# Sums of the looked-up feed-forward weights: from POOL's additions to accumulating DMAs in SBUF

## The chip, the core and the metric

The kernel runs on one core of one Trainium2 chip. The metric is the device time of one execution in microseconds (us), shorter is better.

## What is computed

One transformer block on x, 1024 tokens of 256 channels: a layer norm, attention with 16 heads of 128 and linear position penalties (ALiBi), and beside it a feed-forward part whose three weight matrices are looked up in a table of 16 values.

```python
def _ghost_linear(x, idx, lut):
    w = lut[idx]                                  # int codes 0..15 -> weights
    return jnp.einsum('bsh,oh->bso', x, w)

xn = _layernorm(x)
qkv = xn @ qkv_w + qkv_b
scores = einsum(q, k) + alibi_mask                # causal
ctx = softmax(scores) @ v
attn = ctx @ out_w + out_b
h = silu(_ghost_linear(xn, lut, gate_idx)) * _ghost_linear(xn, lut, up_idx)
return x + attn + _ghost_linear(h, lut, down_idx)
```

## The kernel before

All products are made with three matmuls of float32r parts: a value is split into a rounded part ("hi", made by ACT) and the rest ("lo", made by DVE, or by POOL for weights and for some probabilities). So each tile passes ACT and then DVE or POOL before PE can use it.

Heads are worked two at a time: `pair(n, kind)` with p = 0 and p = 1, the first pair and the last written out, the six between in a hardware loop. A head has eight steps i = 0..7, one for each tile of 128 query rows. At step i PE makes the scores of tile i (L559), DVE masks them and finds the maximum (`mask`, L924, called mask i below), ACT takes the exponential (`exp`, L734) and DVE inverts the row sum (`invert`, L961). Rows 0 to 3 of tiles are scaled by POOL (`norm`, L1112), with a small addition into `pad` ahead of each (L1117), and turned by PE. Tiles 4 to 7 (the upper ones) are scaled by ACT (L750), transposed in 32 x 32 blocks by DVE (`turn_blocks`, L967), and moved between partitions by 16 DMAs on SP's queue (`move`, L400). They are used in the next head: at its steps 4 and 5 ACT makes their hi part in four chunks (`upper_hi_of`, L753) and POOL their lo part (`upper_lo_of`, L1121), and PE multiplies them with v at step 7 ("_pv1", L538).

Nothing is scheduled at run time: each engine executes its own list in the order in which the program writes it, and waits on semaphores. The table UNITS says at which step each projection stands; the constants ending in _AT say at which step the smaller jobs stand.

The feed-forward weights `w_ffn` (128 x 4352 float32) are the sum over the 16 table entries e of (codes == e) * table[e]. Head number e adds entry e, in four parts of 1088 columns. DVE makes the product of a part (`look_up`, L942) in the steps of TERM_AT, for head 0 straight into `w_ffn`, for the others into `term`, of which there is one buffer. POOL adds `term` to the part in the steps of SUM_AT (L1153) and counts `term_added`. The next look-up waits for that count, since it overwrites `term`. The finished weights are split by ACT (L798) and POOL (L1157) at the end of the last head and in the tail, where the feed-forward matmuls run (gate_up and down, L633 and L675).

```python
TERM_AT = (1, 3, 5, 7)
SUM_AT = (1, 3, 6, 7)
...
                    dve.wait_ge(term_added, n * (2 * TERMS) + (p - 1) * TERMS + part)
...
                            pool.wait_ge(term_ready, n * (2 * TERMS) + p * TERMS + part + 1)
...
                            pool.tensor_tensor(piece, piece, term[:, :], ALU.add).then_inc(term_added, 1)
```

Of the kernel before, what the change touches and what calls it, by code (L numbers as in the profile page):

```python
# [29 lines left out]
P = 128  # L30
# [17 lines left out]
TERM_AT = (1, 3, 5, 7)  # L48
SUM_AT = (1, 3, 6, 7)
# [115 lines left out]
def block_ffn(nc, x, w_qk, w_v, w_o, b_qkv, b_out, lut, idx, out):  # L165
    with ExitStack() as ctx:
# [31 lines left out]
        pad = sb("pad", [P, 4 * NT + 1])  # L198
# [492 lines left out]
        def _(act):  # L691
# [13 lines left out]
            act.activation(pad[:, 4 * NT:], eps[:, :], ACT.Sqrt)  # L705
# [6 lines left out]
            act.activation(pad[:, 4 * NT:], eps[:, :], ACT.Exp)  # L712
# [85 lines left out]
            def ffn_w_hi_of(piece):  # L798

                at, width = piece_of(piece)  # L800
                reached = -(-(at + width) // LUT_PIECE)
                act.wait_ge(term_added, (HEADS - 2) * TERMS + reached)
                act.activation(ffn_w(0, at, width), w_ffn[:, at:at + width],
                               ACT.Copy).then_inc(ffn_w_hi, 1)
# [3 lines left out]
            def silu_of(u):  # L808
                act.wait_ge(gate_up_done, u + 1)
                if u < 2:  # L810
                    act.wait_ge(term_added, (HEADS - 1) * TERMS)
                else:
                    act.wait_ge(h_ready, u - 1)
                rows = rows_of(u)
                act.activation(silu_tile(u)[rows, :], ps_s[rows, u % 2, 0:HALF], ACT.Silu).then_inc(silu_done, 1)
# [7 lines left out]
            act.activation(pad[:, 4 * NT:], eps[:, :], ACT.Silu)  # L823
# [20 lines left out]
        def _(dve):  # L844
# [97 lines left out]
            def look_up(n, kind, p, part):  # L942
# [10 lines left out]
                else:  # L953
                    dve.wait_ge(term_added, n * (2 * TERMS) + (p - 1) * TERMS + part)
# [125 lines left out]
        def _(pool):  # L1080
# [39 lines left out]

            def upper_lo_of(n, p, chunk):  # L1121
# [6 lines left out]
            def pair(n, kind):  # L1128
                for p in range(2):
                    for i in range(NT):  # L1130
                        if 1 <= i <= QT:
                            norm(n, p, i - 1)
                        if i in (4, 5) and not (kind == FIRST and p == 0):
# [82 lines left out]
```

## Time and profile before

| | |
|---|---|
| median of 3 runs | 543.18 us (539.96 to 543.33) |
| the profiled execution | 543.26 us |
| its span, first to last instruction | 541.5 us |
| mean granted TensorE clock | 0.987 |
| busy: PE, DVE, POOL, ACT | 493.8, 414.2, 403.6, 360.9 us |

The profile is of one execution. Busy time of an engine is the time in which one of its instructions runs; waits are the idle time ahead of an instruction, with what ended it. A timeline lists an engine's instructions by their start in us from the span's begin. Overlapping instructions of one kind are merged into one row with a count.

### The profile page before, as it was taken

The page shows a single profiled execution, that of the slowest core. Times are in us where ns is not written, and L with a number is a line of the kernel's source. Part 1 is how long each engine was busy: PE and PEld are TensorE (multiplying, and loading weights), DVE is VectorE, ACT ScalarE, POOL GpSimd, SP SyncE. Part 2 cuts the span into 40 slices and gives each one's busy share as a digit, 9 for nine tenths or more (in the row PEclk, how much of TensorE's full clock was granted, in tenths as well). Part 3 has the DMA queues.
Part 4 walks back from the last instruction along what each step waited for, and adds up shares of the span by engine and source line. Part 5 has one row for each costly group of instructions (what it writes and reads, how often), then busy time and mean ns, then how long its engine had stood idle before and what let it go on. Part 6 is the DMA issues. An engine that isn't in the chain of part 4 may idle for free.

```text
span 541.5 us, 9700 instructions
## 1 busy us (share of the span) xinstructions
PE 493.8 (91%) x2826; PEld 422.4 (78%) x2826; DVE 414.2 (76%) x1067; ACT 360.9 (67%) x657; POOL 403.6 (75%) x312
## 2 busy tenths in 40 slices
PE   7896797999889988998899989997999989789998
PEld 6785576898779876987689768986798779578897
DVE  6796988788888878888788987888788886543541
ACT  3575867687767867595959685877678766824430
POOL 5533989788978998798969897889789979921400
PEclk9997999999999999999999999999999999979999
DMA  8204243332514070606160524134331514000001
GB/s 285 87 0 101 62 98 103 73 91 53 146 44 116 13 186 4 156 0 161 38 144 16 119 80 113 47 79 120 70 90 43 119 38 104 0 1 2 0 21 58
DMA packets 18948, 41.65 MB, mean 77 GB/s; under 512 B 4848, under 2 KB 7024, under 8 KB 18800
## 3 DMA queue, kind: packets, MB, share of 16 engines
q1 hardware_dynamic: 18928, 41.40, 30.2%
q8 instruction: 10, 0.16, 0.1%
q14 instruction: 10, 0.08, 0.1%
HBM read 11.83 MB, written 1.05 MB: 24 GB/s over the span
## 4 chain that ended last, share of the span: by engine, by line
POOL 44%; PE 23%; issue 21%; DVE 7%; ACT 3%; DMA 1%; POOLq 0%; DVEq 0%; ACTq 0%
POOL p_t_lo L1125 17%; POOL w_ffn L1153 15%; POOL work L1118 5%; PE ps_u L447 5%; PE ps_u L449 4%; PE ps_u L448 4%; DVE term L958 3%; PE ps_s L447 2%; PE ps_s L448 2%; PE ps_s L449 2%; POOL v_w_lo L1102 2%; POOL pad L1117 2%; POOL qk_w_lo L1097 2%; ACT ctx_t_hi L721 1%; DVE ctx_t_lo L898 1%
## 5 line engine op out<-in xcount | busy, mean ns | idle before, releaser
L1153 POOL TENSOR_TENSOR w_ffn<-w_ffn,term 128x1088 f32<-128x1088 f32 x60 | 155.0, 2584 | 45.4 <-DVE term L958 45.4
L1125 POOL TENSOR_TENSOR p_t_lo<-p_t_lo,p_t_hi 128x1024 fp32r<-128x1024 f32 (+2 forms) x60 | 133.1, 2251 | 0.0
L738 ACT ACTIVATE work<-work,neg_max 128x128 f32<-128x128 f32 (+7 forms) x128 | 99.0, 773 | 24.1 <-DVE neg_max L937 22.1
L937 DVE CUSTOM_DVE_ANT_0 work<-ps_s,alibi 128x128 f32<-128x128 f32 (+7 forms) x128 | 95.8, 749 | 0.0
L447 PE MATMUL ps_u<-p_t_hi,v_hi 128*128 128x512 f32 x192 | 70.5, 367 | 17.7 <-POOL p_t_lo L1125 17.4
L975 DVE STREAM_TRANSPOSE blocks<-work 128x512 f32<-128x512 f32 x120 | 65.3, 582 | 11.6 <-ACT work L750 11.6
L447 PE MATMUL ps_s<-k_hi,q_hi 128*128 128x256 f32 (+2 forms) x192 | 67.3, 350 | 5.3 <-DVE neg_max L937 5.3
L958 DVE TENSOR_SCALAR term<-codes,entry,table 128x1088 f32<-128x1088 uint8 x60 | 65.8, 1096 | 4.3 <-POOL w_ffn L1153 4.3
L449 PE MATMUL ps_u<-p_t_hi,v_lo 128*128 128x512 f32 x192 | 67.2, 350 | 0.0
L448 PE MATMUL ps_u<-p_t_lo,v_hi 128*128 128x512 f32 x192 | 67.0, 349 | 0.0
L448 PE MATMUL ps_s<-k_lo,q_hi 128*128 128x256 f32 (+2 forms) x192 | 65.8, 343 | 0.0
L449 PE MATMUL ps_s<-k_hi,q_lo 128*128 128x256 f32 (+2 forms) x192 | 65.8, 343 | 0.0
L447 PEld LDWEIGHTS ps_u<-p_t_hi,v_hi 128*128 128x128 f32 x192 | 36.3, 189 | 36.0 <-POOL p_t_lo L1125 27.0
L750 ACT ACTIVATE work<-work,inv_sum 128x640 f32<-128x640 f32 (+1 forms) x64 | 61.1, 978 | 0.0
L447 PE MATMUL ps_u<-xn_t_hi,qk_w_hi 128*128 128x512 f32 x128 | 53.7, 419 | 1.4 <-DVE xn_t_lo L882 0.9
L756 ACT ACTIVATE p_t_hi<-p_t_lo 128x1024 fp32r<-128x1024 f32 (+2 forms) x60 | 53.4, 940 | 1.2 <-DMA p_t_lo<-blocks 1.2
L982 DVE TENSOR_TENSOR p_t_lo<-ps_t,p_t_hi 128x128 fp32r<-128x128 f32 (+2 forms) x72 | 34.7, 487 | 21.7 <-ACT p_t_hi L744 21.5
L449 PE MATMUL ps_u<-xn_t_hi,qk_w_lo 128*128 128x512 f32 x128 | 50.7, 396 | 0.0
L448 PE MATMUL ps_u<-xn_t_lo,qk_w_hi 128*128 128x512 f32 x128 | 50.7, 396 | 0.0
L591 PE MATMUL ps_t<-ident,work 128*128 128x128 f32 x186 | 33.4, 284 | 15.0 <-POOL work L1118 10.4
L447 PEld LDWEIGHTS ps_s<-k_hi,q_hi 128*128 128x128 f32 x192 | 36.4, 190 | 10.3 <-DVE neg_max L937 7.2
L721 ACT ACTIVATE q_hi<-ps_u,bias_now 128x512 fp32r<-128x512 f32 x32 | 22.1, 689 | 29.9 <-PE ps_u L449 29.8
(148 smaller groups left out, 1271.1 us busy)
## 6 DMA issues: line engine op xcount, KB each, us to landing
p_t_lo<-blocks SPq DMA_DIRECT2D x240, 116.0 KB, 2.3
qk_raw<-w_qk SPq DMA_DIRECT2D x16, 256.0 KB, 2.7
w_ffn<-idx SPq DMA_DIRECT2D x1, 2176.0 KB, 11.0
v_raw<-w_v SPq DMA_DIRECT2D x8, 256.0 KB, 3.5
o_raw<-w_o SPq DMA_DIRECT2D x8, 256.0 KB, 2.9
out<-acc SPq DMA_DIRECT2D x8, 128.0 KB, 1.7
acc<-x SPq DMA_DIRECT2D x2, 256.0 KB, 3.0
acc<-x SPq DMA_DIRECT2D x1, 512.0 KB, 5.0
```

What stands on the lines that cost most here:

```text
L447: pe.matmul(out, lhs[0], rhs[0], start=first, stop=False)
L448: pe.matmul(out, lhs[0], rhs[1], start=False, stop=False)
L449: return pe.matmul(out, lhs[1], rhs[0], start=False, stop=last)
L738: act.activation(slot(i), slot(i), ACT.Exp, bias=neg_max[:, col:col + 1], scale=-1.0, accum_out=row_sum[:, col:col + 1]).then_inc(exp_done, 1)
L750: act.activation(slot(i), slot(i), ACT.Copy, scale=inv_sum[:, col:col + 1]).then_inc(upper_normed, 1)
L756: act.activation(chunk_rows(0, chunk), chunk_rows(1, chunk).bitcast(F32), ACT.Copy).then_inc(upper_hi, 1)
L937: dve.tensor_tensor_reduce(slot(i).rearrange("p (b c) -> p b c", b=banks), made_of, alibi[:, p, S - width:S].rearrange("p (b c) -> p b c", ...
L958: dve.tensor_scalar(target, codes[:, piece], column(entry, n, p), column(table, n, p), ALU.is_equal, ALU.mult).then_inc(term_ready, 1)
L975: last = dve.transpose(to, slot(i)[:, at:at + count * P].rearrange("p (j a c) -> p j a c", j=count, c=B32))
L982: dve.tensor_tensor(p_rows(1, i, g), turned_rows(i, g), p_rows(0, i, g).bitcast(F32), ALU.subtract).then_inc(p_lo, 1)
L1125: pool.tensor_tensor(rows, rows.bitcast(F32), chunk_rows(0, chunk).bitcast(F32), ALU.subtract).then_inc(upper_lo, 1)
L1153: pool.tensor_tensor(piece, piece, term[:, :], ALU.add).then_inc(term_added, 1)
```

## The change

POOL's 60 additions of `term` to `w_ffn` go. In their place POOL issues a DMA for each, which reads `term` and adds it to the part of `w_ffn` where it lies, and counts 16 into `term_added` on landing. Ahead of the DMA stands an addition of one column into `pad`, which carries the wait for `term_ready`. All counts of `term_added` grow by 16. POOL's wait for the sum of the head before is gone. DVE's look-ups stand at steps 0, 2, 4, 6 and the sums at 1, 3, 5, 7, and a sum's place within a step is now ahead of the upper chunks and of the lo part of q's and k's weights. `pad` grows by four columns, and ACT's small activations name their one column.

```diff
-TERM_AT = (1, 3, 5, 7)
-SUM_AT = (1, 3, 6, 7)
+TERM_AT = (0, 2, 4, 6)
+SUM_AT = (1, 3, 5, 7)
...
-                    dve.wait_ge(term_added, n * (2 * TERMS) + (p - 1) * TERMS + part)
+                    dve.wait_ge(term_added, n * (32 * TERMS) + (p - 1) * (16 * TERMS) + 16 * part)
...
+            def add_term(n, p, part):
+
+                pool.wait_ge(term_ready, n * (2 * TERMS) + p * TERMS + part + 1)
+                pool.tensor_tensor(pad[:, 4 * NT + 1 + part:4 * NT + 2 + part], entry[:, 0:1], entry[:, 0:1], ALU.add)
+                pool.dma_start(w_ffn[:, part * LUT_PIECE:(part + 1) * LUT_PIECE], term[:, :],
+                               accum_op=ALU.add).then_inc(term_added, 16)
...
+                        if i in SUM_AT and not (kind == FIRST and p == 0):
+                            add_term(n, p, SUM_AT.index(i))
                         if i in (4, 5) and not (kind == FIRST and p == 0):
...
-                        elif i in SUM_AT:
-                            part = SUM_AT.index(i)
-                            pool.wait_ge(term_ready, n * (2 * TERMS) + p * TERMS + part + 1)
-                            if kind != FIRST:
-                                pool.wait_ge(term_added, n * (2 * TERMS) + (p - 2) * TERMS + part + 1)
-                            piece = w_ffn[:, part * LUT_PIECE:(part + 1) * LUT_PIECE]
-                            pool.tensor_tensor(piece, piece, term[:, :], ALU.add).then_inc(term_added, 1)
```

How the instructions now stand is shown at three places of a steady pair's head with p = 0. ISA and REGISTER_ALU rows only set a register.

POOL, steps 4 to 7. `pad` ahead of `work` and `work` 128x512 are the scaling of tile 3, `p_t_lo` the chunks, `w_ffn` the sum. Before:

```order
L1117 TENSOR_TENSOR pad<-entry 128x1 [waits inv_ready]
L1118 TENSOR_SCALAR work<-work,inv_sum 128x512
L1123 REGISTER_ALU
L1125 TENSOR_TENSOR p_t_lo<-p_t_lo,p_t_hi 128x4x256 [waits upper_hi]
L1123 REGISTER_ALU
L1125 TENSOR_TENSOR p_t_lo<-p_t_lo,p_t_hi 128x4x256 [waits upper_hi]
L1123 REGISTER_ALU
L1125 TENSOR_TENSOR p_t_lo<-p_t_lo,p_t_hi 128x4x224 [waits upper_hi]
L1125 TENSOR_TENSOR p_t_lo<-p_t_lo,p_t_hi 128x4x160 [waits upper_hi]
L1096 ISA
L1097 TENSOR_TENSOR qk_w_lo<-qk_raw,qk_w_hi 128x512 [waits qk_w_hi]
L1149 REGISTER_ALU
```

Now:

```order
L1118 TENSOR_SCALAR work<-work,inv_sum 128x512
L1130 REGISTER_ALU
L1132 TENSOR_TENSOR p_t_lo<-p_t_lo,p_t_hi 128x4x256 [waits upper_hi]
L1130 REGISTER_ALU
L1132 TENSOR_TENSOR p_t_lo<-p_t_lo,p_t_hi 128x4x256 [waits upper_hi]
L1123 REGISTER_ALU
L1124 TENSOR_TENSOR pad<-entry 128x1 [waits term_ready]
L1125 DMA w_ffn<-term 128x1088
L1130 REGISTER_ALU
L1132 TENSOR_TENSOR p_t_lo<-p_t_lo,p_t_hi 128x4x224 [waits upper_hi]
L1132 TENSOR_TENSOR p_t_lo<-p_t_lo,p_t_hi 128x4x160 [waits upper_hi]
L1096 ISA
```

Before, all four chunks stand ahead of the sum of part 2 (whose rows follow the last one shown). Now its small addition and its DMA stand between the second chunk and the third.

DVE, steps 6 and 7: the transposes of tile 4's blocks, the lo part of a turned tile, and mask 7 (`work,neg_max`, 128x1024). Before:

```order
L975 STREAM_TRANSPOSE blocks<-work 128x4x4x32 [waits blocks_moved]
L975 STREAM_TRANSPOSE blocks<-work 128x4x32
L981 REGISTER_ALU
L982 TENSOR_TENSOR p_t_lo<-ps_t,p_t_hi 128x4x128 [waits p_hi]
L926 REGISTER_ALU
L934 MEMSET pad 128x1 [waits p_turned,scores_done]
L937 ISA work,neg_max<-ps_s,alibi 128x1024
L937 ISA neg_max 128x1
```

Now:

```order
L975 STREAM_TRANSPOSE blocks<-work 128x4x4x32 [waits blocks_moved]
L975 STREAM_TRANSPOSE blocks<-work 128x4x32
L981 REGISTER_ALU
L982 TENSOR_TENSOR p_t_lo<-ps_t,p_t_hi 128x4x128 [waits p_hi]
L954 REGISTER_ALU
L958 TENSOR_SCALAR term<-codes,entry,table 128x1088 [waits term_added]
L926 REGISTER_ALU
L934 MEMSET pad 128x1 [waits p_turned,scores_done]
L937 ISA work,neg_max<-ps_s,alibi 128x1024
L937 ISA neg_max 128x1
```

The look-up of part 3, which waits for `term_added`, now stands directly ahead of mask 7.

DVE, steps 2 and 3: mask 2 has run, `k_lo` is the next head's k, and 128x512 is mask 3. Before:

```order
L965 RECIPROCAL inv_sum<-row_sum 128x1 [waits exp_done]
L1017 REGISTER_ALU
L892 REGISTER_ALU [waits bias_ready]
L898 SCALAR_TENSOR_TENSOR k_lo<-ps_u,bias_now,k_hi 128x512 [waits unit_hi]
L934 MEMSET pad 128x1 [waits blocks_turned,scores_done]
L937 ISA work,neg_max<-ps_s,alibi 128x512
L937 ISA neg_max 128x1
L965 RECIPROCAL inv_sum<-row_sum 128x1 [waits exp_done]
L981 REGISTER_ALU
```

Now:

```order
L965 RECIPROCAL inv_sum<-row_sum 128x1 [waits exp_done]
L1017 REGISTER_ALU
L892 REGISTER_ALU [waits bias_ready]
L898 SCALAR_TENSOR_TENSOR k_lo<-ps_u,bias_now,k_hi 128x512 [waits unit_hi]
L954 REGISTER_ALU
L958 TENSOR_SCALAR term<-codes,entry,table 128x1088 [waits term_added]
L934 MEMSET pad 128x1 [waits blocks_turned,scores_done]
L937 ISA work,neg_max<-ps_s,alibi 128x512
L937 ISA neg_max 128x1
L965 RECIPROCAL inv_sum<-row_sum 128x1 [waits exp_done]
```

The look-up of part 1 stands ahead of mask 3; before, mask 3 followed the lo part of k at once.

## Rows read from the trace of the kernel before

**Rows 1.** The page, busy time by engine, and the groups of instructions, POOL's costliest.
```profile
PE 493.8 (91%) x2826; PEld 422.4 (78%) x2826; DVE 414.2 (76%) x1067; ACT 360.9 (67%) x657; POOL 403.6 (75%) x312
...
L1153 POOL TENSOR_TENSOR w_ffn<-w_ffn,term 128x1088 f32<-128x1088 f32 x60 | 155.0, 2584 | 45.4 <-DVE term L958 45.4
```

**Rows 2.** Windows of one pair of heads each: from:to, length, busy time by engine, clock, DMA.
```profile
82.60:139.70 57.10, 53.42 (x308) 45.76 (x308) 47.37 (x125) 41.94 (x76) 49.66 (x37) 1.00 0.36 88
...
196.80:253.80 57.00, 53.43 (x308) 45.73 (x308) 47.33 (x125) 41.90 (x76) 49.59 (x37) 1.00 0.35 85
```

**Rows 3.** Waits in the pair 196.8 to 253.8: us in all, times, longest.
```profile
PE ps_u L447 <- POOL p_t_lo L1125: 1.9, 3, 1.2
PE ps_t L591 <- POOL work L1118: 1.4, 1, 1.4
```

**Rows 4.** Timeline of ACT, same pair: start, us, instruction (exp 4, upper hi twice).
```profile
199.31 0.82 ACT L738 ACTIVATE work<-work,neg_max 128x640 f32<-128x640 f32 x1
...
200.12 2.00 ACT L756 ACTIVATE p_t_hi<-p_t_lo 128x1024 fp32r<-128x1024 f32 x2
...
229.57 1.99 ACT L756 ACTIVATE p_t_hi<-p_t_lo 128x1024 fp32r<-128x1024 f32 x2
```

**Rows 5.** Timeline of POOL, same pair, and its chunk group by shape.
```profile
227.44 2.94 POOL L1153 TENSOR_TENSOR w_ffn<-w_ffn,term 128x1088 f32<-128x1088 f32 x1 [1.38 <-DVE term L958]
...
231.15 8.92 POOL L1125 TENSOR_TENSOR p_t_lo<-p_t_lo,p_t_hi 128x1024 fp32r<-128x1024 f32 x4
...
248.89 0.20 POOL L1117 TENSOR_TENSOR pad<-entry 128x1 f32<-128x1 f32 x1
249.06 0.37 POOL L1118 TENSOR_SCALAR work<-work,inv_sum 128x128 f32<-128x128 f32 x1
...
L1125 POOL TENSOR_TENSOR p_t_lo<-p_t_lo,p_t_hi 128x1024 fp32r<-128x1024 f32 x30 | 78.8, 2649 | 0.0
```

**Rows 6.** Timeline of DVE, same pair: look-ups (L958), masks (L937), inverse, acc, alibi.
```profile
203.60 1.91 DVE L958 TENSOR_SCALAR term<-codes,entry,table 128x1088 f32<-128x1088 uint8 x1
...
207.91 1.21 DVE L937 CUSTOM_DVE_ANT_0 work<-ps_s,alibi 128x1024 f32<-128x1024 f32 x1
...
217.71 0.28 DVE L937 CUSTOM_DVE_ANT_0 work<-ps_s,alibi 128x128 f32<-128x128 f32 x1
...
237.43 1.22 DVE L937 CUSTOM_DVE_ANT_0 work<-ps_s,alibi 128x1024 f32<-128x1024 f32 x1
...
245.03 1.28 DVE L958 TENSOR_SCALAR term<-codes,entry,table 128x1088 f32<-128x1088 uint8 x1
246.24 0.28 DVE L937 CUSTOM_DVE_ANT_0 work<-ps_s,alibi 128x128 f32<-128x128 f32 x1
...
247.47 0.15 DVE L965 RECIPROCAL inv_sum<-row_sum 128x1 f32<-128x1 f32 x1
...
251.15 0.68 DVE L937 CUSTOM_DVE_ANT_0 work<-ps_s,alibi 128x512 f32<-128x512 f32 x1
...
252.16 0.69 DVE L990 TENSOR_TENSOR acc<-ps_u,acc 128x512 f32<-128x512 f32 x1
252.77 0.84 DVE L958 TENSOR_SCALAR term<-codes,entry,table 128x1088 f32<-128x1088 uint8 x1
253.53 0.89 DVE L1032 TENSOR_SCALAR alibi<-alibi 128x1024 f32<-128x1024 f32 x1
254.35 0.81 DVE L937 CUSTOM_DVE_ANT_0 work<-ps_s,alibi 128x640 f32<-128x640 f32 x1
```

**Rows 7.** Timeline of SP's queue: the 16 moves of one head.
```profile
244.60 10.05 SPq L408 DMA_DIRECT2D p_t_lo<-blocks  x16
```

**Rows 8.** DMA issues: name, queue, count, KB each, median us from issue to landing.
```profile
p_t_lo<-blocks SPq DMA_DIRECT2D x240, 116.0 KB, 2.3
...
w_ffn<-idx SPq DMA_DIRECT2D x1, 2176.0 KB, 11.0
```

**Rows 9.** A window of 2 us in the moves: the last two are DMA share, GB/s.
```profile
218.80:220.80 2.00, 2.00 (x11) 1.70 (x10) 1.61 (x10) 1.18 (x3) 2.00 (x3) 1.00 0.78 178
```

More of the change, by code:

```diff
@@ L197, in block_ffn @@
         entry = sb("entry", [P, LUT])
-        pad = sb("pad", [P, 4 * NT + 1])
+        pad = sb("pad", [P, 4 * NT + 5])
         neg_max = sb("neg_max", [P, 2 * NT])
@@ L704, in _ @@
             act.wait_ge(made, 1)
-            act.activation(pad[:, 4 * NT:], eps[:, :], ACT.Sqrt)
+            act.activation(pad[:, 4 * NT:4 * NT + 1], eps[:, :], ACT.Sqrt)
             root(0)
@@ L711, in _ @@
             xn_hi_of(0, (1,))
-            act.activation(pad[:, 4 * NT:], eps[:, :], ACT.Exp)
+            act.activation(pad[:, 4 * NT:4 * NT + 1], eps[:, :], ACT.Exp)
             def hi_of(n, p, name, bank, no):
@@ L801, in ffn_w_hi_of @@
                 reached = -(-(at + width) // LUT_PIECE)
-                act.wait_ge(term_added, (HEADS - 2) * TERMS + reached)
+                act.wait_ge(term_added, 16 * ((HEADS - 2) * TERMS + reached))
                 act.activation(ffn_w(0, at, width), w_ffn[:, at:at + width],
@@ L810, in silu_of @@
                 if u < 2:
-                    act.wait_ge(term_added, (HEADS - 1) * TERMS)
+                    act.wait_ge(term_added, 16 * ((HEADS - 1) * TERMS))
                 else:
@@ L821, in h_hi_of @@
                 act.activation(h_tile(0, u)[rows, :], h_raw(u)[rows, :], ACT.Copy).then_inc(h_hi_done, 1)
-            act.activation(pad[:, 4 * NT:], eps[:, :], ACT.Silu)
+            act.activation(pad[:, 4 * NT:4 * NT + 1], eps[:, :], ACT.Silu)
             units = number(PAIRS - 1, LAST, 1, "pv0")
```

## Prediction, made before the changed kernel had run

> **What bounds the kernel now.** I read the page's totals and groups first. PE is busy 91% of the span, DVE 76%, POOL 75%, and POOL's costliest group is the one the change removes: 60 sums of a term, 2584 ns each, 155.0 us in all [rows 1]. The reader is to see that 155 us of POOL is not 155 us of the kernel. So I cut the span into its repeating stretch: from one lo part of v's weights (L1102) to the next is one pair of heads, 57.0 or 57.1 us, and two such pairs have the same busy times on every engine [rows 2]. PE is busy 53.4 of the 57.0. In the waits of one pair PE waits 1.9 us for the upper chunks' lo parts (L1125) and 1.4 us for POOL's scaled rows (L1118) [rows 3]. That is all that a free POOL could give back directly: 3.3 us a pair.
>
> Then I followed one head to the next in the timelines. At step 4 ACT starts the hi part of the upper chunks, at 200.12 and at 229.57 us [rows 4]. At step 7 DVE masks the last tile (mask 7: 207.91 and 237.43) [rows 6]. ACT's exp and the scaling, DVE's transposes of the blocks, and 16 moves from SP's queue (10.05 us of issuing from 244.60, 2.3 us to land) [rows 7, 8] lead to the next head's chunks. The last of them is issued by 254.65, so it lands by 257.0 at the latest, and the next hi part starts at 200.12 + 57.0 = 257.1, right behind exp 4 (199.31, 0.82 us) [rows 4]. So this circle from head to head is nearly as tight as PE: upper hi -> mask 7 takes 7.86 and 7.79 us, mask 7 -> next upper hi 19.7 (into the head with p = 0) and 21.7 (into that with p = 1). Together 57.0.
>
> **What the change removes.** Eight POOL sums a pair, 8 x 2.58 = 20.7 us, of which two delay the row scaling in front of the chunks (one runs 227.44 to 230.38, and the chunk after it starts 0.6 us late at 231.15) [rows 5]. It also takes DVE's look-up at step 7 (1.28 us at 245.03, 0.84 where nothing else runs) from the way to mask 0 [rows 6]. If nothing came in their place, PE's 3.3 us a pair would be the gain.
>
> **What it adds.** The order shows two new places. On POOL the issue of part 2 stands behind chunks 0 and 1. On DVE the look-up of part 3 now stands straight ahead of mask 7, and it waits for part 2 to have landed, since there is one term buffer. The look-up of part 1 stands likewise ahead of mask 3, behind part 0. In before neither mask waits for a sum. Call A the time from POOL taking up the DMA to its landing.
>
> Upper hi -> mask 7 becomes: chunk 0's hi part 1.0 (half of 2.00) [rows 4], two chunks at 2.65 = 5.3 and the small add 0.2 [rows 5], A, look-up 0.84: 7.34 + A, where it was 7.8. DVE had other work up to 7.0, so it stands still for A - 0.5.
>
> Mask 7 -> upper hi, into p = 0, counted from 237.43: without the look-up at 245.03 mask 0 starts at 7.6. The lo part of q waits for PE and ACT as before, then the look-up of part 0 stands there: inverse 0, at 10.0 in before (247.47), comes at 10.5. POOL's small add and row scaling take 0.55 and the second small add 0.2 [rows 5]: 11.3. Then A. Look-up 0.84, mask 3 0.7 to 0.8, inverse and lo part of tile 0 0.4, the sum into acc 0.7, the alibi product 0.9, mask 4 0.8 [rows 6], exp 4 until the hi part 0.8 [rows 4]: 16.4 + A. Into p = 1 mask 0 came 9.8 after mask 7, comes 9.1 now, inverse 0 at 12.3, and by the same steps 18.2 + A. The moves alone would give 257.0 - 237.4 = 19.6, later only if A is under 3.2.
>
> A pair is then 2 x 7.34 + 16.4 + 18.2 + 4A = 49.3 + 4A, against 57.0. It breaks even at A = 1.93 us.
>
> **The size of A.** No row shows an accumulating transfer or one issued by POOL. From below: a move, 116 KB from SBUF to SBUF, lands 2.3 us after issue [rows 8]; with 0.3 for POOL, 2.6. By size: the change's DMA has 544 KB, 8 rows of 4352 bytes for each of 16 engines. While the moves run, the engines are 0.78 busy at 178 GB/s [rows 9], so one busy engine moves 14.3 GB/s: the move's 7.4 KB on each engine take 0.5 us, 34.8 KB take 2.4, and landing comes to 2.3 + 1.9 = 4.2. The largest load, 2176 KB, took 11.0 [rows 8]; a quarter of it is 2.8 us, not far from the 2.4. From above: an accumulation must read its target too; doubling the data gives 2.3 - 0.5 + 4.8 = 6.6, and sharing with the moves, which run just when parts 0 and 1 are issued, adds to it. Below nothing is excluded, since the look-up waits for the landing whatever it costs. I take 4.2, by the nearest row in kind (SBUF to SBUF), and keep 2.6 and 6.7 as ends.
>
> The Trainium skill ("DMA: Bandwidth & Descriptors", Anatomy of one DMA — SWDGE path) gives about 2.0 us fixed plus bytes over 436 GB/s for a DMA issued by GpSimd: as an estimate 3.3 us here, a pair of 62.4 and a time of about 584. No run here shows it for an accumulation.
>
> **Sum.** A = 4.2 gives a pair of 66.1, 9.1 more (9.0 by the unrounded 57.1). There are 15 heads with chunks, so 14 intervals, and the piece ahead of the first and behind the last make about one more half: 7.5 pairs. 7.5 x 9.0 = 67.5 us. The profiled execution has a span of 541.5 and 543.26 us in all; the median of the three runs is 543.18, so nothing is shifted. 543.3 + 67.5 = 610.8, so 611. At A = 2.6 a pair is 59.7: 563. At 6.7 it is 76.1: 686. POOL's freed 20.7 us a pair is no term: the queue is in order and POOL's next work waits for the same landings through DVE. The tail changes little: the last pieces wait for all 60 sums in before too.
>
> Where DVE and POOL meet, a look-up beside POOL's chunks took 1.91 us (203.60), against 0.84 alone (252.77) [rows 6]. The DMA's issue on POOL may be held in the same way: one hold by the alibi product (0.89) in every A would add 3.6 us to a pair and 27 to the time. The range has room for that, the forecast doesn't count it.
>
> The Trainium skill ("SBUF — State Buffer", SBUF: two separate sides) says that while DVE runs certain two-port operations GpSimd can't write the descriptors of its own DMAs, so that they look blocked. It speaks against this change. The row of 1.91 us agrees that the two engines hold each other up, though it shows it for arithmetic only, and by the rule A would be longer, never shorter.
>
> **Rivals.**
> - *The landings are hidden* (faster). If A is under 1.9, say because POOL's queue hands the DMA off at once and it runs in the 0% stretches of the DMA engines, the waits of PE for POOL go: 57.0 - 3.3 = 53.7 a pair, 7.5 x 3.3 = 25, so 518. For it: part 2 and part 3 are issued when no move runs. Against it: the moves, with a fifth of the bytes, need 2.3 us [rows 8]. Chance 0.07.
> - *Break-even*: A about 2, or DVE's stall falls on time it spends waiting for ACT anyway: 543. Chance 0.04.
> - *The accumulation is the bound itself*: A about 7, from reading the target and from sharing with the moves. A pair is 77.3, and 543 + 7.5 x 20.3 = 695. PE would stand still for several us a head, and its clock, granted at 1.00 in the pairs [rows 2], might fall. For it: the engines are 0.78 busy where parts 0 and 1 are issued [rows 9]. Against it: part 2 and part 3 have the engines to themselves. Chance 0.14.
> - *The change doesn't free POOL*: if issuing holds POOL as long as the sum did (2.6 us), A is 2.6 + 4.2 less the 0.3 counted, 6.5, and the time 679. It is the lower edge of the case above and counted there.
>
> **The numbers.** Forecast 0.75, for 563 to about 670; the heavy rival 0.14; faster 0.07; break-even 0.04. Faster by over 1% 0.07, within 1% 0.04, slower by over 1% 0.89 (1% is about what a measurement of this kernel can tell from no change). The range 562 to 686 leaves out the faster and even cases and a part of the heavy one, some 2 in 10.
>
> **What would show it.** In the profile after: a steady pair of about 66 us; DVE waiting before L958 for the DMA into w_ffn, most before mask 7 and mask 3, 3 to 4 us each; the time of that DMA from issue to landing near 4; POOL at under 60% of the span, its wait now for upper_hi and term; PE idle some 12 us a pair. Wrong: a landing under 2 us, a DVE that waits for the DMA less than 5 us a pair, or a pair under 57 us with PE's waits for POOL gone. If a pair is over 60 us but DVE doesn't wait for the DMA, the loop is another than I say.

## The result, and the profile after

The changed kernel takes 658.4 us (median of four runs, 657.2 to 660.0) against 542.9 us for the kernel before (four runs, 540.0 to 543.3). The ratio is 1.214, with a 95% interval from 1.210 to 1.219: 115.5 us slower. The forecast was 611, slower by 67.5 us, with a range from 562 to 686.

The page of the changed kernel, its totals and then the two groups that belong to the change; they answer to [rows 1]:

```profile
PE 528.9 (80%) x2826; PEld 455.6 (69%) x2826; DVE 414.5 (63%) x1067; ACT 358.1 (54%) x657; POOL 311.3 (47%) x372
...
L958 DVE TENSOR_SCALAR term<-codes,entry,table 128x1088 f32<-128x1088 uint8 x60 | 67.1, 1118 | 109.4 <-DMA w_ffn<-term 109.4
...
L1125 POOL DMA_DIRECT2D w_ffn<-term x60 | 51.9, 865 | 0.2 <-issue 0.2
```

POOL's 155.0 us of sums are gone, and 51.9 us of issuing stand in their place. POOL fell from 403.6 to 311.3 us of work, and the span grew by 115.8 us. The reader is to see the middle row: DVE stood still for 109.4 us in front of its look-ups until a DMA had landed. Before, it stood there for 4.3 us, on POOL. That one group is nearly as large as the whole loss, though a wait is a loss only if it lies in the circle from head to head; the experiments below are about that.

Two steady pairs, windows as in [rows 2] (length, busy by engine, clock, DMA share, GB/s):

```profile
165.70:237.50 71.80, 59.00 (x324) 50.75 (x323) 47.61 (x128) 43.56 (x81) 38.20 (x46) 0.93 0.63 136
237.50:309.40 71.90, 57.67 (x311) 49.57 (x310) 47.38 (x124) 41.65 (x77) 37.64 (x44) 0.93 0.59 125
```

These pairs take 71.8 and 71.9 us instead of 57.0, with nearly the same instructions (where a window is cut moves a few in or out). From the first upper hi to the last, seven pairs, the time grew from 398.5 to 499.6 us: 101.1 us, or 14.4 a pair. Another 9.6 us came ahead of the first (67.64 against 58.00) and 5.1 behind the last. PE is idle for 14.2 us of the second pair, and its granted clock is 0.93 where it was 1.00. How long the transfers take (KB each, median us from issue to landing; [rows 8]):

```profile
w_ffn<-term POOLq DMA_DIRECT2D x60, 544.0 KB, 4.7
p_t_lo<-blocks SPq DMA_DIRECT2D x240, 116.0 KB, 2.3
```

These medians hide two kinds. Parts 2 and 3 land 4.6 to 4.7 us after the issue (once 5.0), while part 0, issued beside the moves, takes 5.6 to 7.0 us and part 1 4.7 to 7.3. Of a head's 16 moves, three or four land only after more than 3.5 us, up to 5.6 in the steady pair.

And the circle itself in the pair from 237.5. POOL first, then DVE's look-ups and the masks that end each section; they answer to [rows 5] and [rows 6]. The head with p = 0 ends with the mask at 258.98, the one with p = 1 with that at 296.08:

```profile
235.11 0.86 POOL L1125 DMA_DIRECT2D w_ffn<-term  x1
...
247.47 4.69 POOL L1132 TENSOR_TENSOR p_t_lo<-p_t_lo,p_t_hi 128x1024 fp32r<-128x1024 f32 x2 [0.96 <-ACT p_t_hi L756]
...
252.96 0.88 POOL L1125 DMA_DIRECT2D w_ffn<-term  x1
...
273.28 0.83 POOL L1125 DMA_DIRECT2D w_ffn<-term  x1
...
290.60 0.87 POOL L1125 DMA_DIRECT2D w_ffn<-term  x1
```

```profile
241.81 0.85 DVE L958 TENSOR_SCALAR term<-codes,entry,table 128x1088 f32<-128x1088 uint8 x1 [4.69 <-DMA w_ffn<-term]
...
250.29 2.46 DVE L958 TENSOR_SCALAR term<-codes,entry,table 128x1088 f32<-128x1088 uint8 x1 [3.75 <-DMA w_ffn<-term]
...
258.01 1.04 DVE L958 TENSOR_SCALAR term<-codes,entry,table 128x1088 f32<-128x1088 uint8 x1
258.98 1.21 DVE L937 CUSTOM_DVE_ANT_0 work<-ps_s,alibi 128x1024 f32<-128x1024 f32 x1
...
279.58 0.85 DVE L958 TENSOR_SCALAR term<-codes,entry,table 128x1088 f32<-128x1088 uint8 x1 [2.42 <-DMA w_ffn<-term]
...
287.23 1.01 DVE L958 TENSOR_SCALAR term<-codes,entry,table 128x1088 f32<-128x1088 uint8 x1 [2.19 <-DMA w_ffn<-term]
...
295.31 0.84 DVE L958 TENSOR_SCALAR term<-codes,entry,table 128x1088 f32<-128x1088 uint8 x1 [1.12 <-DMA w_ffn<-term]
296.08 1.22 DVE L937 CUSTOM_DVE_ANT_0 work<-ps_s,alibi 128x1024 f32<-128x1024 f32 x1
```

From a DMA on POOL to the look-up behind its landing: part 0 takes 6.3 us (273.28 to 279.58) and, in the other head of the pair, 6.7 (235.11 to 241.81); part 2 takes 5.05 (252.96 to 258.01) and 4.71 (290.60 to 295.31). Behind part 3 DVE never waits. These four places are those of the four A in the prediction, but only three of them are waits for the landing. In front of 258.01 DVE doesn't wait: part 2 had landed 4.71 us after its issue, at 257.67, and DVE was late itself. In that head, with p = 0, the look-up of part 2 first waits 3.75 us for part 1 to land, then meets POOL's chunks (247.47 to 252.16) and takes 2.46 us instead of 0.84, and mask 5 stands behind it.

Over all 60 look-ups DVE waits 46.9 us ahead of mask 3 (for part 0), 51.4 us ahead of mask 5 (for part 1) and 11.2 us ahead of mask 7 (for part 2); of the last, 9.5 us are in the heads with p = 1.

### The profile page after: what moved, and what is told of

It reads as the page before. It is cut to its first block, busy times and chain, and to the rows that moved or that the text cites. A ratio compares the mean times of both kernels' runs of the same rounds, so it can differ in the third digit from the quotient of the medians.

```text
span 657.3 us, 9740 instructions
## 1 busy us (share of the span) xinstructions
PE 528.9 (80%) x2826; PEld 455.6 (69%) x2826; DVE 414.5 (63%) x1067; ACT 358.1 (54%) x657; POOL 311.3 (47%) x372
## 4 chain that ended last, share of the span: by engine, by line
issue 35%; DMA 17%; PE 16%; POOL 16%; ACT 7%; DVE 6%; SPq 2%; DVEq 0%; POOLq 0%; ACTq 0%
DMA w_ffn<-term 16%; POOL p_t_lo L1132 5%; POOL qk_w_lo L1097 3%; POOL w_ffn L1125 2%; PE ps_u L447 2%; PE ps_s L447 2%; PE ps_s L448 2%; PE ps_s L449 2%; ACT work L750 2%; ACT p_t_hi L756 2%; SPq L408 2%; PE ps_u L449 2%; PE ps_u L448 2%; POOL work L1118 2%; ACT work L738 2%
## 5 line engine op out<-in xcount | busy, mean ns | idle before, releaser
L958 DVE TENSOR_SCALAR term<-codes,entry,table 128x1088 f32<-128x1088 uint8 x60 | 67.1, 1118 | 109.4 <-DMA w_ffn<-term 109.4
L447 PE MATMUL ps_s<-k_hi,q_hi 128*128 128x256 f32 (+2 forms) x192 | 75.4, 393 | 67.0 <-DVE neg_max L937 67.0
L1117 POOL TENSOR_TENSOR pad<-entry 128x1 f32<-128x1 f32 x64 | 15.0, 234 | 180.0 <-DVE inv_sum L965 179.4
L937 DVE CUSTOM_DVE_ANT_0 work<-ps_s,alibi 128x128 f32<-128x128 f32 (+7 forms) x128 | 96.2, 751 | 0.0
L447 PEld LDWEIGHTS ps_s<-k_hi,q_hi 128*128 128x128 f32 x192 | 40.6, 211 | 77.7 <-DVE neg_max L937 74.1
L447 PE MATMUL ps_u<-xn_t_hi,qk_w_hi 128*128 128x512 f32 x128 | 57.7, 451 | 24.5 <-DVE ctx_t_lo L898 23.5
L975 DVE STREAM_TRANSPOSE blocks<-work 128x512 f32<-128x512 f32 x120 | 65.3, 582 | 11.5 <-ACT work L750 11.5
L448 PE MATMUL ps_s<-k_lo,q_hi 128*128 128x256 f32 (+2 forms) x192 | 71.9, 375 | 0.0
L449 PE MATMUL ps_s<-k_hi,q_lo 128*128 128x256 f32 (+2 forms) x192 | 71.7, 373 | 0.0
L750 ACT ACTIVATE work<-work,inv_sum 128x640 f32<-128x640 f32 (+1 forms) x64 | 60.9, 975 | 0.0
L756 ACT ACTIVATE p_t_hi<-p_t_lo 128x1024 fp32r<-128x1024 f32 (+2 forms) x60 | 53.3, 936 | 6.4 <-DMA p_t_lo<-blocks 6.4
L449 PE MATMUL ps_u<-xn_t_hi,qk_w_lo 128*128 128x512 f32 x128 | 54.7, 427 | 0.0
L1125 POOL DMA_DIRECT2D w_ffn<-term x60 | 51.9, 865 | 0.2 <-issue 0.2
L447 PE MATMUL ps_u<-v_w_hi,xn_t_hi 128*128 128x256 f32 x128 | 39.0, 305 | 12.1 <-DVE ctx_t_lo L898 10.3
L447 PEld LDWEIGHTS ps_u<-xn_t_hi,qk_w_hi 128*128 128x128 f32 x128 | 27.0, 211 | 29.9 <-issue 22.8
```

The lines of the kernel that those rows point to most:

```text
L447: pe.matmul(out, lhs[0], rhs[0], start=first, stop=False)
L448: pe.matmul(out, lhs[0], rhs[1], start=False, stop=False)
L449: return pe.matmul(out, lhs[1], rhs[0], start=False, stop=last)
L750: act.activation(slot(i), slot(i), ACT.Copy, scale=inv_sum[:, col:col + 1]).then_inc(upper_normed, 1)
L756: act.activation(chunk_rows(0, chunk), chunk_rows(1, chunk).bitcast(F32), ACT.Copy).then_inc(upper_hi, 1)
L937: dve.tensor_tensor_reduce(slot(i).rearrange("p (b c) -> p b c", b=banks), made_of, alibi[:, p, S - width:S].rearrange("p (b c) -> p b c", ...
```

## The experiments

All are compared with runs of the kernel before in the same series. Where no number of runs is given, the time is that of a single run, and a few us mean nothing: the kernel before gave 542.5 in one series, 550.1 in another (one run each), and 542.4 to 551.3 in the eleven runs of a third (median 544.1).

**Less in each transfer: copy, half, and next to nothing.** The first leaves the addition out (a term overwrites w_ffn), the second and third the other columns of the later terms.

```
e1_copy    -  accum_op=ALU.add
e2_half    -  w_ffn[..1088 columns], term[:, :]    +  w_ffn[..544 columns], term[:, 0:544]
e10_tiny   -  w_ffn[..1088 columns], term[:, :]    +  w_ffn[..32 columns], term[:, 0:32]
```

> The DMAs copy the term over the part of w_ffn instead of adding it, so the weights come out as the last term alone. Same bytes written, same waits, same places. Theory (the head-to-head circle waits for each landing, 4 landings a pair, 7.5 pairs, so 30 us of time for each 1 us of landing): the landing falls from 4.7 us by what reading the target costs, 1.2 to 2.4 us, and the time from 658 to 585 to 625. Rival (the adding costs nothing, the landing is set by bytes of the term and the fixed part): 4.7 us and 650 to 660. Rival (the DMA engines' share, not the wait, is what costs): the time falls in proportion to the DMA's packets' share, by more than 30 us for each us of landing.

Measured: 616.0 us (before 542.5). The theory held. The landing fell from 4.7 to 3.0 us: the addition costs 1.7 us of landing (and 0.27 us of POOL at each issue, 865 against 594 ns), and 42 us of time, 25 for each us of landing where 30 were reckoned. DVE's waits halved to 52.3 us.

> Each accumulating DMA adds only the first half of the columns of its part (272 KB instead of 544 KB), so half of the sums is left out. Waits and places stay. Theory: data is some 2.9 of the 4.7 us, the landing falls to 3.2 or 3.3 us and the time by 4 x 7.5 x 1.45 = 43 us to about 615. Rival (the fixed part of a landing is nearly all of it): landing over 4.2 us, time over 640.

Measured: 630.2 us, landing 3.3 us, DVE waits 52.8 us. The landing came as expected, the time 15 us later than expected. The waits fell by 56.6 us, the time only by 28.

> The changed kernel with each accumulating DMA cut to 32 of its 1088 columns (16 KB in place of 544 KB; the other columns of the later terms are left out). All waits stay, the traffic goes. Theory (a landing has a fixed part near the 2.2 us of the smallest moves, and the rest of its 4.7 us grows with the bytes): a landing of 2.0 to 2.6 us, DVE waits 20 to 45 us in all before its look-ups, 585 to 605 us. Rival A (bytes alone cost): landing under 1.5 us and 575 us or less. Rival B (the wait for any DMA costs, whatever its size): landing over 3 us and 610 us or more.

Measured: 607.0 us (before 544.1), landing 2.1 us, DVE waits 18.9 us. The landing was as the theory said, the waits 1 us below its range and the time 2 us above, so the numbers came nearly right. But the reason was another. With 16 KB the waits for DMAs had almost gone, and 63 us of the loss were still there. The group of look-ups shows where:

```profile
L958 DVE TENSOR_SCALAR term<-codes,entry,table 128x1088 f32<-128x1088 uint8 x60 | 85.3, 1421 | 52.3 <-DMA w_ffn<-term 52.3
```

```profile
L958 DVE TENSOR_SCALAR term<-codes,entry,table 128x1088 f32<-128x1088 uint8 x60 | 96.0, 1599 | 19.6 <-DMA w_ffn<-term 18.9
```

The first of these is e1_copy, the second e10_tiny; the changed kernel's row, 67.1 and 109.4, stands above. As the wait shrinks, the look-ups themselves grow, from 1118 ns to 1599 in the mean. In e10_tiny's timeline it is, in seven of the eight heads with p = 1, the look-up of part 3, at step 6 (4.2 to 4.3 us each); with p = 0 it is that of part 2 (1.5 to 2.9 us), behind a wait for part 1. DVE, and POOL beside it:

```profile
265.65 4.27 DVE L958 TENSOR_SCALAR term<-codes,entry,table 128x1088 f32<-128x1088 uint8 x1
269.85 1.21 DVE L937 CUSTOM_DVE_ANT_0 work<-ps_s,alibi 128x1024 f32<-128x1024 f32 x1
```

```profile
264.16 3.94 POOL L1132 TENSOR_TENSOR p_t_lo<-p_t_lo,p_t_hi 128x896 fp32r<-128x896 f32 x2
267.77 1.55 POOL L1097 TENSOR_TENSOR qk_w_lo<-qk_raw,qk_w_hi 128x512 fp32r<-128x512 f32 x1
```

The look-up is taken up at 265.65 and ends at 269.92, 0.6 us after POOL's row (chunks 2 and 3, then qk_lo) ends at 269.32. Alone it takes 0.84 us. Mask 7 stands behind it. The prediction knew of one hold of 1.91 us [rows 6] and left it out of the forecast. As I read it, a long landing hides a part of the hold, because the look-up then more often comes when POOL has nothing to do; a short landing lays it bare. With a landing of 2.1 us the formula gives some 548 us and the run took 607, so the time isn't linear in A, and no break-even near A = 1.93 shows in this order. Between landings of 4.7 and 2.1 us lie 51 of the 115.5 us.

That POOL's instructions are what holds a look-up can be read in all runs. In the 13 kernels with this form of look-up, 226 look-ups took over 1.1 us, and every one of them ended 0.57 to 0.61 us after a POOL instruction had ended.

**Is it that form of instruction?** e12_three_operands is e10_tiny with another form of look-up:

```
-  dve.tensor_scalar(target, codes[..], column(entry), column(table), is_equal, mult)
+  dve.scalar_tensor_tensor(target, codes[..], column(entry), column(table).to_broadcast([P, LUT_PIECE]), is_equal, mult)
```

> The kernel e10_tiny (607 us) with the look-up written as an instruction with three operands (the table's entry as a broadcast tensor) in place of the one with two; the result of each look-up is the same. Alone it should take longer than the 0.84 us of the old form: the three-operand instruction of 512 columns takes 0.74 us before, so some 1.4 us for 1088. Theory (the old form, and only that form, must wait until POOL's row of instructions leaves the way to SBUF that the two share): the look-up of part 3 at step 6 takes 1.3 to 1.6 us in every head, not 4.3 us, no look-up of all 60 takes over 1.8 us, and the time falls to 580 to 602 us although the sum over the 60 look-ups changes little. Rival A (the look-up is slow because POOL's traffic slows every DVE instruction in its way): it still takes 3.5 us or more, and the time rises to 615 us or more. Rival B (the held look-up lies beside other work and costs nothing): the row changes as the theory says and the time does not fall.

Measured in four runs: 636.5 us, 1.170 times before (1.166 to 1.175), 29 us slower than the one run of e10_tiny. The theory fell. The new form takes 1.34 us alone; 0.5 us more in each of 60 look-ups are 30 us, so this run puts no price on the hold. But it shows that the new form is held too, longer than the old one:

```profile
279.25 4.83 DVE L958 SCALAR_TENSOR_TENSOR term<-codes,entry,table 128x1088 f32<-128x1088 uint8 x1 [0.87 <-DMA w_ffn<-term]
```

```profile
277.79 3.89 POOL L1133 TENSOR_TENSOR p_t_lo<-p_t_lo,p_t_hi 128x896 fp32r<-128x896 f32 x2
281.39 1.52 POOL L1098 TENSOR_TENSOR qk_w_lo<-qk_raw,qk_w_hi 128x512 fp32r<-128x512 f32 x1
```

It ends at 284.08, 1.17 us behind POOL's row (282.91), and one of the 60 took 7.9 us. Rival A's numbers came true, but not its reason, as not every DVE instruction is slow beside POOL. In e10_tiny the two subtractions ahead of the held look-up (L982 and L990, which read one operand from PSUM) took their usual 0.69 and 0.68 us while POOL's chunks ran. Nor is it enough that all operands lie in SBUF: the transposes of 128x512 blocks, with one SBUF input, took 0.71 us beside the chunks and 0.67 to 0.71 elsewhere. The Trainium skill ("SBUF — State Buffer", Who interferes with whom) says that a DVE instruction with two SBUF inputs contends with a GpSimd instruction that reads SBUF, as one in a two-port mode does with any; the 4.83 us of the new form, which reads two SBUF tensors, agree with it, and my claim that only the old form is held doesn't. A form of the look-up that isn't held wasn't found.

**The places without the DMA.** e3_places has the changed kernel's places, and POOL adds the terms itself:

```
-  pool.dma_start(w_ffn[part], term[:, :], accum_op=ALU.add).then_inc(term_added, 16)
+  pool.tensor_tensor(w_ffn[part], w_ffn[part], term[:, :], ALU.add).then_inc(term_added, 1)
```

> Only the new places: look-ups at steps 0, 2, 4, 6, sums at 1, 3, 5, 7 and ahead of the upper chunks as in the change, but POOL adds with its own instruction (2.6 us), no DMA. Theory (the circle runs through the sums of parts 0 and 2 whatever makes them): A is 2.6, a pair 49.3 + 4 x 2.6 = 59.7 us, time about 563, range 550 to 575. Rival (the places cost nothing, only the DMA's landing does): 538 to 546.

Measured: 601.1 us (before 542.5). Both numbers were too low, so theory and rival fell: half of the loss is there without any DMA. The sum of part 2 now stands ahead of POOL's chunks 2 and 3, the look-up of part 3 waits for it and is then held by the chunks, and mask 7 is behind both:

```profile
262.79 2.59 DVE L958 TENSOR_SCALAR term<-codes,entry,table 128x1088 f32<-128x1088 uint8 x1 [1.20 <-POOL w_ffn L1126]
265.30 1.21 DVE L937 CUSTOM_DVE_ANT_0 work<-ps_s,alibi 128x1024 f32<-128x1024 f32 x1
```

e7_three_late is e3_places with the look-up of part 3 one step later, behind mask 7 (`TERM_AT = (0, 2, 4, 7)`).

> The kernel with the new places and POOL's own adds (e3_places, 601 us), but the look-up of part 3 at step 7 instead of step 6, so that mask 7 is ahead of it. Theory (in e3_places mask 7 waited behind that look-up, held while POOL ran its chunks): 575 us or less, a pair at 61 us or less. Rival (the cost of the places is in the adds' place ahead of POOL's chunks, which make the multiplication by the upper part late): 590 us or more.

Measured: 632.3 us (before 550.1), worse, so the remedy fell. It doesn't refute the hold: the stretch it aimed at, upper hi -> mask 7, fell from the 12.1 us of e3_places to 7.7 and 7.1. But the stretch from mask 7 to the next upper hi grew from 18.9 and 21.3 us to 23.5 and 30.3, by a new wait. POOL's queue waits 7.15 us for that look-up (pad, before the sum), and the look-up of part 0, now right behind it at step 0, waits for the sum. POOL, and DVE's look-ups of part 3 and of the next head's part 0:

```profile
253.78 0.19 POOL L1124 TENSOR_TENSOR pad<-entry 128x1 f32<-128x1 f32 x1 [7.15 <-DVE term L958]
```

```profile
252.86 0.84 DVE L958 TENSOR_SCALAR term<-codes,entry,table 128x1088 f32<-128x1088 uint8 x1
...
256.61 0.85 DVE L958 TENSOR_SCALAR term<-codes,entry,table 128x1088 f32<-128x1088 uint8 x1 [1.76 <-POOL w_ffn L1126]
```

With a single term buffer, two look-ups as neighbours have nothing to hide the sum between them.

**The DMA in the old places.** e5_oldsteps is the changed kernel with `TERM_AT = (1, 3, 5, 7)`.

> The changed kernel with DVE's look-ups put back to steps 1, 3, 5 and 7; the sums stay accumulating DMAs, issued at steps 1, 3, 5, 7. Theory (the new places cost something of their own, since the look-up of part 3 at step 6 stands ahead of mask 7 and is slowed by POOL's chunks): the time falls from 658 to 590 to 625 us, and the look-up of part 3 lasts 0.84 us instead of 2 us and more. Rival A (only the landing of the DMAs counts): each DMA is issued as long before the next look-up as the steps allow, the landing of 4.7 us is still waited for, and the time stays at 640 us or more. Rival B (the DMA costs nothing where the look-ups stand right): 560 us or less.

Measured: 647.4 us (before 550.1). Rival A held: DVE waits 104.9 us for landings, nearly as long as in the changed kernel, and the landing is now 6.0 us in the median. With the DMA the old steps give back 11 us of the 115.5; the landing finds its way into the circle in both. Here parts 0 and 3 are the slow ones (6.2 and 6.6 us in the median), and part 3's DMA is issued beside the moves.

**The DMA without its wait.** In e4_unhooked the same 544 KB come from another tile (so w_ffn gets other values), and DVE waits for no landing; POOL waits ahead of each DMA for the one to the same part of the head before. e8_unhooked_old has the old steps in addition.

```
-  dve.wait_ge(term_added, ...)
-  pool.dma_start(w_ffn[part], term[:, :], accum_op=ALU.add)
+  pool.dma_start(w_ffn[part], xn_t_lo[1088 columns], accum_op=ALU.add)
```

> All 60 accumulating DMAs run with the same bytes and are issued at the same places, but read a buffer that nobody writes (the lo part of the normed x), so that no look-up waits for a landing; POOL waits ahead of each DMA for the one to the same part of the head before. The weights come out wrong. Theory (the wait of DVE for the landing is the whole cost): 520 to 548, PE's clock back above 0.97. Rival (sharing the DMA engines with the moves, or the hold of POOL's queue by issuing): 580 or more.

Measured: 675.2 us, slower than the changed kernel. My theory that the wait is all fell here. Without the wait the look-up of part 3 runs into POOL's chunks (4.4 to 5.7 us in each of the first 14 heads; 115.8 us over all 60), and the transfers run into the moves: ACT waits 48.8 us for moves, 6.4 in the changed kernel.

> The unhooked kernel (e4_unhooked, 675 us: the DMAs carry the same bytes from another tile and DVE waits for no landing, so the values of the feed-forward weights are not the reference's) with the look-ups back at steps 1, 3, 5, 7. Theory (both the held look-up and the DMA engines' sharing cost): 590 to 640 us, the look-ups at 0.84 us, the moves' issue still at 12 us or more. Rival A (the held look-up is all): 560 us or less. Rival B (the traffic of the DMAs is all): 650 us or more.

Measured: 659.9 us (before 550.1); rival B held. Here the look-ups are shorter again (79.8 us, with that of part 2 held for 2.9 us in nearly every head) and DVE waits for nothing, yet the time is that of the changed kernel. The group of ACT's hi parts shows the new wait, and SP's queue the reason (a move group took 10.05 us in [rows 7]):

```profile
L756 ACT ACTIVATE p_t_hi<-p_t_lo 128x1024 fp32r<-128x1024 f32 (+2 forms) x60 | 53.6, 941 | 108.7 <-DMA p_t_lo<-blocks 108.7
```

```profile
259.57 18.02 SPq L408 DMA_DIRECT2D p_t_lo<-blocks  x16
```

```profile
w_ffn<-xn_t_lo POOLq DMA_DIRECT2D x60, 544.0 KB, 6.8
p_t_lo<-blocks SPq DMA_DIRECT2D x240, 116.0 KB, 4.5
```

The moves are issued in 18.0 us instead of 10.05 and land in 4.5 instead of 2.3, the DMAs from POOL land in 6.8. SP waits for no semaphore between the 16 moves: those issued while a DMA from POOL is under way take up to 2.4 us each to issue instead of 0.6, and land after 4 to 7 us. So the 33 MB of sums and the moves meet in the same stretch. In a steady head 9 to 11 of the 16 moves land later than 3.5 us; in the changed kernel it is three or four, as I read it because DVE's wait spaces the DMAs. Taking the wait away only moves the price: 109 us of DVE became 109 us of ACT.

**No sum at all.** e6_noadd drops POOL's add_term and DVE's wait (the later heads' terms are left out); e9_noadd_old has the old steps in addition.

```
-  add_term(n, p, SUM_AT.index(i))
-  dve.wait_ge(term_added, ...)
```

> The changed kernel without any sum: no DMA, no instruction on POOL in its place, and DVE's look-ups, at steps 0, 2, 4, 6, wait for nothing, so the terms of the later heads are left out of the feed-forward weights. Theory (two costs beside the landing: the look-up of part 3 beside POOL's chunks, and the DMA engines shared with the moves; this kernel has only the first): 545 to 575 us, with the look-up at step 6 at 1.7 us or more and the moves' issue back at 10 us. Rival A (the places cost nothing without POOL's add): 515 to 540 us. Rival B (the places cost all that the changed kernel loses): 600 us or more.

> No sum at all (as e6_noadd, 565 us: the terms of the later heads are left out), with the look-ups back at steps 1, 3, 5, 7. It is the most that any way of taking the sums from POOL could give in the order of before. Theory (POOL's adds are in the circle of a head at the places that the kernel before has, and the new places of the look-ups cost some 15 to 20 us by themselves): 505 to 530 us. Rival (POOL's adds cost nothing in the kernel before, so nothing was to be won by taking them away): 538 to 548 us, and the places cost 20 us. Second rival (the look-ups' steps cost nothing; what e6_noadd lost is the order of POOL's norms ahead of its chunks): 555 us or more.

Measured: 565.0 us (before 550.1) and 558.2 us (before 544.1). The theory of e6 held: the look-up at step 6 took 1.9 to 2.2 us in the first 14 heads, and the moves were issued in 10.1 us. The theory of e9 fell, and its second rival has the number: with 155 us of work taken from POOL and nothing in its place, the kernel isn't faster; this one run is 14 us slower. The look-ups of part 2, at step 5, point to a reason; three heads of e9_noadd_old:

```profile
239.43 2.83 DVE L958 TENSOR_SCALAR term<-codes,entry,table 128x1088 f32<-128x1088 uint8 x1
...
267.68 2.99 DVE L958 TENSOR_SCALAR term<-codes,entry,table 128x1088 f32<-128x1088 uint8 x1
...
298.25 2.82 DVE L958 TENSOR_SCALAR term<-codes,entry,table 128x1088 f32<-128x1088 uint8 x1
```

In the kernel before the same look-up takes 1.91 and 0.93 us in turn (203.60 and 233.24). The short one, which [rows 6] leaves out:

```profile
233.24 0.93 DVE L958 TENSOR_SCALAR term<-codes,entry,table 128x1088 f32<-128x1088 uint8 x1
```

The merged row of [rows 5] holds four chunks of different lengths; the first alone runs from 231.15 to 233.58. The look-up was taken up 0.34 us before that end and got in behind it. In e9_noadd_old the first chunk ends at 267.74; the look-up comes at 267.68, only 0.06 us before, is passed over, and is over at 270.67, 0.58 us after the second chunk (267.69 to 270.09). So it is held for a whole chunk more, and upper hi -> mask 7 takes 8.9 and 9.5 us instead of 7.8. From hi part to hi part most pairs are 58.8 us, two of six 60.3 and 60.9, where before they were 57.1. This is read from rows; no run moved that look-up alone.

**One sum of four as a DMA, in the order of before.** e11_part1 tries to gain something: POOL adds parts 0, 2 and 3, and part 1 is an accumulating DMA at its old place, with a semaphore of its own.

```
   elif i in SUM_AT:
-      pool.tensor_tensor(piece, piece, term[:, :], ALU.add).then_inc(term_added, 1)
+      if part == 1:
+          pool.dma_start(piece, term[:, :], accum_op=ALU.add).then_inc(term_moved, 16)
+      else:
+          pool.tensor_tensor(piece, piece, term[:, :], ALU.add).then_inc(term_added, 1)
```

> The kernel before in its own order, with one of the four sums, that of part 1 (step 3, just ahead of the upper part's subtractions on POOL), as an accumulating DMA issued from POOL at the same place, with a semaphore of its own; POOL adds the other three. Theory (a landing of 4.7 to 5 us fits between this issue and the look-up of part 2 some 6 us later, no moves are under way then, and POOL saves 1.7 us ahead of its chunks in each head): 520 to 538 us, faster than before. Rival A (what POOL saves is not in the circle): 541 to 546 us. Rival B (the landing is late, or delays moves): 550 us or more.

Measured in six runs: 570.8 us, 1.045 times before (1.037 to 1.052). Rival B held, by its late landing and not by the moves, which were issued in 10.1 us. The landing took 5.7 us in the median, DVE waited 13.5 us for it, and the look-ups took 75.7 us in all instead of 65.8: with p = 1 that of part 2 was mostly held for 2.8 us as in e9, and in the last head it took 8.95 us. No version beat the kernel before.

All kernels in one table. Look-ups and waits are sums over the 60 look-ups; the last column is ACT's wait for moves ahead of L756. "Loss" is against before in the same series.

| kernel | us | loss | look-ups | their wait | ACT's wait |
|---|---|---|---|---|---|
| before | 542.9 | | 65.8 | 4.3 | 1.2 |
| changed | 658.4 | 115.5 | 67.1 | 109.4 | 6.4 |
| e1_copy | 616.0 | 73.5 | 85.3 | 52.3 | 5.5 |
| e2_half | 630.2 | 87.8 | 88.5 | 53.0 | 4.0 |
| e3_places | 601.1 | 58.6 | 80.9 | 40.8 | 5.8 |
| e4_unhooked | 675.2 | 132.7 | 115.8 | 0.0 | 48.8 |
| e5_oldsteps | 647.4 | 97.3 | 75.7 | 104.9 | 1.0 |
| e6_noadd | 565.0 | 15.0 | 67.7 | 0.0 | 6.9 |
| e7_three_late | 632.3 | 82.2 | 59.6 | 43.3 | 0.3 |
| e8_unhooked_old | 659.9 | 109.8 | 79.8 | 0.0 | 108.7 |
| e9_noadd_old | 558.2 | 14.0 | 81.5 | 0.0 | 9.7 |
| e10_tiny | 607.0 | 62.9 | 96.0 | 19.6 | 2.3 |
| e11_part1 | 570.8 | 26.6 | 75.7 | 15.2 | 1.2 |
| e12_three_operands | 636.5 | 93.6 | 130.3 | 29.6 | 0.8 |

Add the three last columns and take off the 71.3 of before. The changed kernel gives 111.6 against 115.5 lost, e1 71.8 against 73.5, e3 56.2 against 58.6, e8 117.2 against 109.8, e9 19.9 against 14.0, e12 89.4 against 93.6. In these kernels the look-ups and ACT's wait ahead of its hi part come to nearly the whole loss. It is a tally and no proof, as a wait need not lie in the circle. In e11 it is 6 too small, in e6 12; in e5 it is 13 too large. In four it is much too small: e2 by 14, e10 by 16, e4 by 39, e7 by 50. In e7 it is POOL's queue, as shown; in e4 and the others it isn't settled. The losses of e5 to e8 rest on the one run of 550.1; against the usual 543 each is 7 larger, which would put e8 right, e5 at 6 too large, and e6 and e7 at 19 and 57 too small.

## Why the prediction came out right in kind and short in size

- **Where the time is bound: right.** The circle from head to head, in which POOL's 155 us are no term, was the right picture. A pair grew, nearly all other instructions stayed, and e9, without any sum, took 558 us. The signs it named came too: POOL at 47%, PE idle for 14.2 us of a pair, a landing of 4.7 us.
- **The formula 49.3 + 4A: right in its sum, in part by luck.** With the landings of the pair, 6.67, 6.28, 4.71 and 4.68 us, it gives 71.6, and the pair took 71.9. With p = 1 the step from upper hi to mask 7 is as reckoned: 7.34 + 4.68 = 12.0, measured 11.95. With p = 0 it took 12.6 us, near the 12.05 of the formula, but on another way: through the landing of part 1, the look-up of part 2 held for 2.46 us and mask 5. The waits of 3 to 4 us were foretold ahead of mask 7 and mask 3. Ahead of mask 3 they came (2.42 and 4.69 us in the pair), ahead of mask 7 they were 0 and 1.12, and the largest sum, 51.4 us, stood ahead of mask 5, which it hadn't named.
- **The size of A: the term that was mis-sized.** I took 4.2 from SBUF-to-SBUF moves, with 0.3 of it for POOL. Part 2, with few other transfers about, landed in 4.7; part 0, issued close behind the moves, in 6.7 and 6.3. Together they are 5.5 us a pair over 16.8, nearly the 5.8 by which the pair missed its 66.1. Over the seven pairs that makes 38 us of the 48 that the span was longer than forecast; the other 10 lie at the ends, which took 14.7 us more where half a pair, 4.5, was reckoned. e1_copy splits the landing: 3.0 us for a copy, 1.7 more for the addition. With the addition, 16, 272 and 544 KB land in 2.1, 3.3 and 4.7 us. So the fixed part was about right and the bytes alone were overrated (as an estimate, 3.0 - 2.1 = 0.9 us where 1.9 were put), and the price of the addition, which I had put at the upper end only, was the term to count.
- **The landing by the page's formula** (3.3 us, from "DMA: Bandwidth & Descriptors" of the Trainium skill, Anatomy of one DMA — SWDGE path) was near the copy's 3.0 us, and 1.4 us short for the accumulation.
- **PE's clock: not counted, and its price is open.** I had it falling only in the heavy rival. It fell in the changed kernel as well. In the first of these two windows PE is busy for 0.17 us of 3.00 (it waits 3.1 us for a mask of DVE, which waits for the landing), and in the second the granted clock is 0.50, the level of 1.2 GHz:

```profile
240.50:243.50 3.00, 0.17 (x1) 0.17 (x2) 1.69 (x7) 0.19 (x1) 0.07 (x1) 0.79 0.87 202
243.50:246.50 3.00, 3.00 (x12) 2.90 (x13) 3.00 (x9) 2.45 (x7) 2.96 (x6) 0.50 0.80 229
```

  At 264.5 to 270.5 the mean clock was 0.72 again, and there inverse 0 of the next head came 13.4 us behind mask 7 where 12.3 were reckoned; into the head with p = 0 it was 11.5 (222.72 to 234.23) where 10.5 were reckoned. That is about 2 us a pair, and other steps were some 1 us shorter. No run was made for the clock alone, so its share isn't known.
- **The hold of look-up and POOL: known and left out.** In the changed kernel its sum didn't grow, since the look-ups took 67.1 us in all against 65.8, though with p = 0 it stood, behind the landing of part 1, on the way to mask 7. It speaks against the rival "landings hidden", whose 518 us no run came near: e10_tiny, with landings of 2.1 us, took 607, and without any sum the kernel took 558 to 565. The break-even rival and the lower end of the range, 562 at A = 2.6, left it out as well; e3_places, where POOL itself adds in 2.54 us, took 601. e1_copy gives the same picture: with its landings of 4.5 us for part 0 and 3.0 for part 2 the formula gives 64.3 a pair and about 597 us, and it took 616.
- **The rule that GpSimd can't write descriptors while DVE holds the port** (the Trainium skill, "SBUF — State Buffer", SBUF: two separate sides). No row shows it here: the 60 issues on POOL took 865 ns in the mean and 1007 at the longest.
- **The heavy rival** (A about 7, 695 us) had the price of the addition and the sharing. Its size came only for part 0, 5.6 to 7.0 us, and not for part 2.

## What to carry to other kernels

Before work is moved off an engine, ask whether that engine's queue is in the circle at all; here removing 155 us of POOL's work without any replacement gained nothing and in one run cost 14 us, and the rows suggest that it shifted two engines that hold each other up. A DMA used as an adder has a price of its own: take its landing from a copy of the same bytes and add something for the addition (here 3.0 and 1.7 us), then look which transfers run beside it. Don't trust a median of landings where the places differ: here it was 4.7 us, and part 0 took 6.2. With one buffer between producer and DMA the landing can become a link in the chain several times a head, and unhooking the wait doesn't help where other transfers need the engines in the same stretch.

## What the runs showed of the hardware that I had not expected

- A held DVE instruction doesn't always get in behind the POOL instruction that runs when it arrives. In e10_tiny it sat through the end of two chunks and of one more instruction (4.27 us), in e4_unhooked for 5.67 us in a steady head, in e12 once for 7.9 us and in e11_part1 once for 8.95; in e9_noadd_old it got in after one chunk (2.8 to 3.0 us). What decides between them wasn't found.
- When it does get in, it is in step with POOL: 226 held look-ups in 13 kernels all ended 0.57 to 0.61 us after a POOL instruction's end.
- The accumulation costs POOL too: an issue takes 865 ns with it and 594 as a copy. Halving the columns didn't change it (867).
- Large transfers from POOL's queue slow the issuing on SP's queue, not only the landing: 16 moves took 10.05 us alone, 12.2 in the changed kernel and 18.0 in e8_unhooked_old. With 16 KB in each transfer (e10_tiny) it was 10.1 again.
